# A recurrent two-layer block: scan items of one state by 1024 tokens, the drive in PSUM, C*h on GpSimd, and the experts' product on VectorE

## The reference

```python
# s: inner width 128, 64 states
A = -exp(A_log); delta = softplus(u @ W_delta + b_delta); Bm = u @ W_B; Cm = u @ W_C
def step(h, inputs):                      # u is silu(conv(left half of y @ W_up))
    dA = exp(d_t[..., None] * A)
    h = dA * h + (d_t * u_t)[..., None] * b_t[:, None, :]
    return h, einsum('bdn,bn->bd', h, c_t)
s = x + ((ys + u * D) * silu(right)) @ W_down + b_down
# m: 16 experts; each takes its 512 best tokens of each batch, and one shared expert takes all
h = gelu(x_tok @ Wg) * (x_tok @ Wu); eo = (h @ Wd) * topk_w   # scattered and added
```

## Time and profile before

| | us |
|---|---|
| median of 3 runs | 4562.25 |
| lowest and highest | 4562.19, 4566.79 |
| the profiled execution | 4572.77 |
| its span | 4571.0 |

### The profile page before, as it was taken

How to read it: one execution, slowest core, us unless ns; L and a number is a source line. 1 busy time by engine, 2 the same in 40 slices (tenths; PEclk the granted TensorE clock), 3 DMA queues, 4 the chain that set the end, 5 groups by cost and what they waited for, 6 DMA issues and landing times. The chain is left out here.

```text
span 4571.0 us, 63922 instructions
## 1 busy us (share of the span) xinstructions
PE 4084.4 (89%) x22996; PEld 3215.1 (70%) x22996; DVE 3323.2 (73%) x4687; ACT 2541.6 (56%) x4869; POOL 2382.1 (52%) x1652
## 2 busy tenths in 40 slices
PE   8899999979999999789999866689998999899975
PEld 7799999967899999656666545556666666566653
DVE  5466666655666666438788889888788787878777
ACT  6644444446444444367766643366666766666654
POOL 3100000032000000147667639789899998989887
PEclk9999999989999999899999858899999999999986
DMA  2010000010000000125444322455555565556568
GB/s 86 22 33 24 20 24 23 24 48 32 29 24 20 24 23 24 55 98 159 142 153 153 117 78 71 116 164 152 166 174 164 158 172 157 166 154 171 159 185 311
DMA packets 242095, 465.67 MB, mean 102 GB/s; under 512 B 33905, under 2 KB 154482, under 8 KB 241778
## 3 DMA queue, kind: packets, MB, share of 16 engines
q1 hardware_dynamic: 217202, 428.01, 29.2%
q0 software_dynamic: 24576, 33.57, 4.0%
HBM read 392.16 MB, written 69.34 MB: 101 GB/s over the span
## 5 line engine op out<-in xcount | busy, mean ns | idle before, releaser
L1560 POOL TENSOR_TENSOR scan_drive_sb<-scan_b_wide_sb,scan_du_sb 128x1024 f32<-128x1024 f32 x512 | 1304.7, 2567 | 241.4 <-DVE scan_h_sb L1472 234.7
L1472 DVE TENSOR_TENSOR_SCAN scan_h_sb<-decay_bank,scan_state_sb,scan_drive_sb 128x512 f32<-128x512 f32 x896 | 1107.7, 1267 | 135.8 <-ACT decay_bank L1810 125.8
L1810 ACT ACTIVATE decay_bank<-scan_delta_sb,a_neg_sb 128x512 f32<-128x512 f32 x1024 | 699.0, 686 | 263.8 <-DVE scan_h_sb L1472 261.0
L1479 DVE TENSOR_TENSOR scan_ch_sb<-c_pair,scan_h_sb 128x1024 f32<-128x1024 f32 x512 | 616.3, 1204 | 155.3 <-PE c_pair L1647 152.6
L1658 PEld LDWEIGHTS y_bank<-identity_sb,scan_ch_sb 128*128 128x128 f32 x4096 | 542.3, 151 | 191.1 <-issue 107.1
L1658 PE MATMUL y_bank<-identity_sb,scan_ch_sb 128*128 128x128 f32 x4096 | 641.3, 288 | 3.8 <-ACT scan_temp_sb L1828 3.8
L977 PE MATMUL ybank<-v_low_hi_lo_sb,pt_hi_b_sb 128*128 128x384 f32 x2048 | 622.1, 340 | 9.6 <-DVE pt_lo_b_sb L859 9.6
L912 POOL TENSOR_TENSOR acc_b_sb<-acc_b_sb,g_in_b_sb 128x256 f32<-128x256 f32 x64 | 47.2, 738 | 1101.2 <-DVE acc_b_sb L895 1101.2
L1647 PE MATMUL c_pair<-scan_cc_sb,select_state_sb 128*128 128x512 f32 x1024 | 445.1, 518 | 186.2 <-DVE scan_ch_sb L1479 185.3
L1014 ACT ACTIVATE p_b_sb<-scores,softmax_cols_b_sb 128x1024 f32<-128x1024 f32 x256 | 285.7, 1116 | 533.1 <-DVE softmax_cols_b_sb L853 395.9
L978 PE MATMUL ybank<-v_low_hi_lo_sb,pt_lo_b_sb 128*128 128x256 f32 x2048 | 574.2, 280 | 0.0
(11 more groups left out here) (302 smaller groups left out, 8112.7 us busy)
## 6 DMA issues: line engine op xcount, KB each, us to landing
scan_b_wide_sb<-b_scratch SPq DMA_DIRECT2D x512, 512.0 KB
x_b_sb<-x SPq DMA_DIRECT2D x16, 512.0 KB, 4.1
x_res_b_sb<-x SPq DMA_DIRECT2D x64, 128.0 KB, 2.3
g_in_b_sb<-g_scratch SPq DMA_DIRECT2D x64, 128.0 KB, 2.2
x_scratch<-x_res_b_sb SPq DMA_DIRECT2D x64, 128.0 KB, 1.7
xn_scratch<-xn_out_b_sb SPq DMA_DIRECT2D x64, 128.0 KB, 1.7
scan_xn_sb<-xn_scratch SPq DMA_DIRECT2D x16, 512.0 KB
moe_x_sb<-xn_scratch SPq DMA_DIRECT2D x16, 512.0 KB, 5.6
```

What stands on the lines that cost most here:

```text
L1472: e.tensor_tensor_scan(k.h[i % H_BUFFERS][:, j, :], k.decay_banks[S % DECAY_BANKS][:, :], k.drive[i % DRIVE_BUFFERS][:, j, :], start, ALU. ...
L1479: e.tensor_tensor(k.ch[i % CH_BUFFERS][:, :, :], k.c_bank[:, :, :], k.h[i % H_BUFFERS][:, :, :], ALU.mult).then_inc(k.s_ch, 1)
L1560: e.tensor_tensor(k.drive[i % DRIVE_BUFFERS][:, :, :], k.b_wide[i % B_BUFFERS][:, :, :], k.du[c % 2][:, :].unsqueeze(1).broadcast_to([P, P ...
L1810: e.activation(k.decay_banks[S % DECAY_BANKS][:, :], k.delta[c % 2][:, :], ACT.Exp, scale=wt.a[:, n:n + 1]).then_inc(k.s_decay, 1)
```

## The change

- An item is now one state of 1024 tokens (`WIDE`, two chunks): again 512 items, 64 per wide. Both chunks of a wide are prepared before its items begin.
- PE broadcasts B, no longer C: `broadcast_b(i + 1)` writes 1024 columns into one of two PSUM tiles of two banks each (`DRIVE_BANKS`), once the scan of item `i - 1` is over. DVE multiplies them in place by `delta * u` (`drive`) and runs one scan of 1024 columns, with the drive in PSUM and the decay in SBUF (three buffers, one exp of 1024 columns each). POOL does C*h (`read_out(i - 1)`), with C from DRAM, loaded two items ahead. PE's eight transposes of an item stand together.
- DVE makes the experts' product, with up read from PSUM; ACT's copy of the up part and POOL's product are gone, and h has two buffers.
- The projections of the scan use unsplit fp32 weights, one matmul for three, which removes the instructions that made the lower parts on ACT, DVE and POOL.
- The last two groups, not one, are finished after the scan; the others may come before. `down` runs for the two halves five steps apart.

```diff
+HALVES = 2
+WIDE = HALVES * CHUNK
+WIDES = ALL_CHUNKS // HALVES
+WIDES_OF = CHUNKS // HALVES
 INNER = 128
 STATES = 64
-PAIR = 2
-LAG = 2
-AHEAD = 2
-PAIRS = STATES // PAIR
-ITEMS = ALL_CHUNKS * PAIRS
+ITEMS = WIDES * STATES
+LAG = 3
...
-DECAY_BANKS = 3
+DECAY_BUFFERS = 3
+DRIVE_BANKS = 2
 H_BUFFERS = 3
 CH_BUFFERS = 2
-B_BUFFERS = 3
-DRIVE_BUFFERS = 3
-B_AHEAD = 4
+C_BUFFERS = 3
+C_AHEAD = 2
...
+def halves(prepare, W):
+    for half in range(HALVES):
+        yield from prepare(HALVES * W + half)
+
+
+def down_steps(step, W):
+
+    for s in range(DOWN_STEPS):
+        for half in range(HALVES):
+            if 0 <= s - HALF_LAG * half < HALF_STEPS:
+                step(HALVES * W + half, s - HALF_LAG * half)
+        yield
...
-        if 0 <= i - 1 < ITEMS:
-            broadcast_c(i - 1)
-        if 0 <= i + AHEAD < ITEMS:
-            drive(i + AHEAD)
-        for j in range(PAIR):
-            S = PAIR * i + j
-            if 0 <= S + 2 < PAIR * ITEMS:
-                decay(S + 2)
-            if 0 <= S < PAIR * ITEMS:
-                recur(S)
-            if 0 <= S - PAIR * LAG < PAIR * ITEMS:
-                add_up(S - PAIR * LAG)
-            if j == 0:
-                helpers.step()
-                yield
+            if m == LAG + C_AHEAD + 1 and W + 1 < WIDES:
+                helpers.ahead = halves(prepare, W + 1)
+            load_c(i + C_AHEAD)
+        if 0 <= i + 1 < ITEMS:
+            broadcast_b(i + 1)
+            decay(i + 1)
+        if 0 <= i < ITEMS:
+            drive(i)
+        helpers.step()
+        yield
+        if 0 <= i < ITEMS:
+            recur(i)
         if 0 <= i - 1 < ITEMS:
             read_out(i - 1)
             keep(i - 1)
-        if 0 <= i - LAG < ITEMS:
-            c, m = divmod(i - LAG, PAIRS)
-            if m == PAIRS - 1:
-                helpers.down.insert(0, down(c))
+        if 0 <= i - LAG + 1 < ITEMS:
+            add_up(i - LAG + 1)
+            W, m = divmod(i - LAG + 1, STATES)
+            if m == STATES - 1:
+                for half in range(HALVES):
+                    y_out(HALVES * W + half)
+                helpers.down.append(down_steps(down, W))
...
+    def load_c(i):
+        W, n = divmod(i, STATES)
+        w.wait_ge(k.s_c_saved, 16 * HALVES * (W + 1))
+        w.wait_ge(k.s_ch, i - C_BUFFERS + 1)
+        e.dma_start(k.c_wide[i % C_BUFFERS][:, :], c_dram[W][n, :].partition_broadcast(P)).then_inc(k.s_c[i % C_BUFFERS], 16)
...
-    def recur(S):
-        i, j = divmod(S, PAIR)
-        c, n = divmod(S, STATES)
-        w.wait_ge(k.s_decay, S + 1)
+    def drive(i):
+        W, n = divmod(i, STATES)
+        bank = k.drive_banks[i % DRIVE_BANKS][:, :]
+        w.wait_ge(k.s_b, i + 1)
+        w.wait_ge(k.s_du, HALVES * (W + 1))
+        e.tensor_tensor(bank, bank, k.du[W % 2][:, :], ALU.mult).then_inc(k.s_drive, 1)
+
+    def recur(i):
+        W, n = divmod(i, STATES)
+        w.wait_ge(k.s_decay, i + 1)
         w.wait_ge(k.s_drive, i + 1)
         w.wait_ge(k.s_kept, i - H_BUFFERS + 1)
         w.wait_ge(k.s_ch, i - H_BUFFERS + 1)
-        start = 0.0 if c % CHUNKS == 0 else k.state[:, n:n + 1]
-        e.tensor_tensor_scan(k.h[i % H_BUFFERS][:, j, :], k.decay_banks[S % DECAY_BANKS][:, :], k.drive[i % DRIVE_BUFFERS][:, j, :], start,
+        start = 0.0 if W % WIDES_OF == 0 else k.state[:, n:n + 1]
+        e.tensor_tensor_scan(k.h[i % H_BUFFERS][:, :], k.decay[i % DECAY_BUFFERS][:, :], k.drive_banks[i % DRIVE_BANKS][:, :], start,
                              ALU.mult, ALU.add).then_inc(k.s_scan, 1)
-
-    def read_out(i):
-        w.wait_ge(k.s_c, i + 1)
-        w.wait_ge(k.s_scan, 2 * (i + 1))
-        w.wait_ge(k.s_y, PAIR * (i - CH_BUFFERS + 1))
-        e.tensor_tensor(k.ch[i % CH_BUFFERS][:, :, :], k.c_bank[:, :, :], k.h[i % H_BUFFERS][:, :, :], ALU.mult).then_inc(k.s_ch, 1)
...
-    def drive(i):
-        c = i // PAIRS
-        w.wait_ge(k.s_b[i % B_BUFFERS], 16 * (i // B_BUFFERS + 1))
-        w.wait_ge(k.s_du, c + 1)
-        w.wait_ge(k.s_scan, PAIR * (i - DRIVE_BUFFERS + 1))
-        e.tensor_tensor(k.drive[i % DRIVE_BUFFERS][:, :, :], k.b_wide[i % B_BUFFERS][:, :, :],
-                        k.du[c % 2][:, :].unsqueeze(1).broadcast_to([P, PAIR, CHUNK]), ALU.mult).then_inc(k.s_drive, 1)
+    def read_out(i):
+        w.wait_ge(k.s_c[i % C_BUFFERS], 16 * (i // C_BUFFERS + 1))
+        w.wait_ge(k.s_scan, i + 1)
+        w.wait_ge(k.s_y, i - CH_BUFFERS + 1)
+        e.tensor_tensor(k.ch[i % CH_BUFFERS][:, :], k.c_wide[i % C_BUFFERS][:, :], k.h[i % H_BUFFERS][:, :], ALU.mult).then_inc(k.s_ch, 1)
...
-            e.matmul(bank, wt.up_hi[:, ci, cols], k.yt_hi[:, ci, :], start=(ci == 0), stop=False)
-            e.matmul(bank, wt.up_hi[:, ci, cols], k.yt_lo[:, ci, :], start=False, stop=False)
-            last = e.matmul(bank, wt.up_lo[:, ci, cols], k.yt_hi[:, ci, :], start=False, stop=(ci == DC - 1))
+            last = e.matmul(bank, wt.up[:, ci, cols], k.yt[:, ci, :], start=(ci == 0), stop=(ci == DC - 1))
...
-    def broadcast_c(i):
-        c, m = divmod(i, PAIRS)
-        fills.wait_emptied(w, "bc", c, 1)
-        w.wait_ge(k.s_ch, i)
-        for j in range(PAIR):
-            n = m * PAIR + j
-            last = e.matmul(k.c_bank[:, j, :], wt.select[:, n:n + 1].broadcast_to([P, P]), k.cc[c % 2][:, :], start=True, stop=True)
-        last.then_inc(k.s_c, 1)
-
-    def add_up(S):
-        i, j = divmod(S, PAIR)
-        c, n = divmod(S, STATES)
+    def broadcast_b(i):
+        W, n = divmod(i, STATES)
+        for half in range(HALVES):
+            fills.wait_emptied(w, "b", HALVES * W + half)
+        w.wait_ge(k.s_scan, i - DRIVE_BANKS + 1)
+        for half in range(HALVES):
+            cols = slice(half * CHUNK, (half + 1) * CHUNK)
+            last = e.matmul(k.drive_banks[i % DRIVE_BANKS][:, cols], wt.select[:, n:n + 1].broadcast_to([P, P]), k.bb[W % 2][:, cols],
+                            start=True, stop=True)
+        last.then_inc(k.s_b, 1)
+
+    def add_up(i):
+        W, n = divmod(i, STATES)
         w.wait_ge(k.s_ch, i + 1)
         if n == 0:
-            w.wait_ge(k.s_y_out, c)
-        for t in range(GT):
+            w.wait_ge(k.s_y_out, HALVES * W)
+        for t in range(HALVES * GT):
...
-    def decay(S):
-        c, n = divmod(S, STATES)
-        w.wait_ge(k.s_delta, c + 1)
-        w.wait_ge(k.s_scan, S - DECAY_BANKS + 1)
-        e.activation(k.decay_banks[S % DECAY_BANKS][:, :], k.delta[c % 2][:, :], ACT.Exp, scale=wt.a[:, n:n + 1]).then_inc(k.s_decay, 1)
+    def decay(i):
+        W, n = divmod(i, STATES)
+        w.wait_ge(k.s_delta, HALVES * (W + 1))
+        w.wait_ge(k.s_scan, i - DECAY_BUFFERS + 1)
+        e.activation(k.decay[i % DECAY_BUFFERS][:, :], k.delta[W % 2][:, :], ACT.Exp, scale=wt.a[:, n:n + 1]).then_inc(k.s_decay, 1)
...
-    def up(q, f):
-        fills.wait_filled(w, "moe_up", q, f)
-        w.wait_ge(k.s_h, HB * (q - 1) + f + 1)
-        e.activation(k.u[f][:, :], fills.bank("moe_up", q, f), ACT.Copy).then_inc(fills.emptied("moe_up", q, f), 1)
...
-    def product(q, f):
-        fills.wait_emptied(w, "moe_up", q, f)
-        w.wait_ge(k.s_gelu, HB * q + f + 1)
-        if q > 0:
-            wait_down(w, fills, q - 1)
-        e.tensor_tensor(k.h[:, f, :], k.u[f][:, :], k.g[f][:, :], ALU.mult).then_inc(k.s_h, 1)
...
+    def product(q, f):
+        fills.wait_filled(w, "moe_up", q, f)
+        w.wait_ge(k.s_gelu, HB * q + f + 1)
+        if q > 1:
+            wait_down(w, fills, q - 2)
+        e.tensor_tensor(k.h[q % 2][:, f, :], fills.bank("moe_up", q, f), k.g[f][:, :], ALU.mult).then_inc(fills.emptied("moe_up", q, f), 1)
...
-        w.wait_ge(k.s_h, HB * (q + 1))
+        wait_hidden(w, fills, q)
...
-LAST = ALL_GROUPS - 1
+LAST = ALL_GROUPS - HALVES
...
-        if g == LAST:
-            yield from no_steps(DOWN_STEPS)
+        while g >= LAST and not pace.scanned:
+            yield
```

493 lines of the change are left out of this document (211 added, 282 removed).

## The result

| | before | after |
|---|---|---|
| median of 4 runs each, us | 4562.22 | 4592.26 |
| lowest and highest | 4559.47, 4566.79 | 4590.19, 4596.14 |
| ratio, 95% interval | | 1.0067, 1.0054 to 1.0079 |

A forecast was written before the change was run, and what follows sets the result against it. No engine was full; engines holding each other up in turn set the pace. Start +44, shared -102, choice 0, routed -113, end +106, tail -12 total -77: span 4494, or 4485 us in the runs' measure, range 4370 to 4600.

The forecast's parts named there:

- The start: Before the first scan: both chunks of the first wide item prepared first, 31 more steps of 1.45 us, +44 us.
- the end: After the routed experts' last scatter: 40 items at 3.5 us plus final-group work and load waits, 174 us against 68, +106.
- the product: Gelu times up, moved to VectorE: next instruction starts 0.61 us later, +2.44 us per block, nothing hides it.
- rival (b): Scan on VectorE: the wide scan saves a fixed 0.2 us per 512-column scan, 102 us less, 4383 us; chance 0.04.
- T in the routed stage: Time of an item beside the routed experts: 41.8 us per block of 9.5 items, 4.4 us each against 4.70.
- the sentence on buffers: Two broadcast banks, three decay buffers, three of h: PE may be one whole item early, where the gain is expected.
- the floor: VectorE's undisturbed time per item, set by the scan: stays 3.48 us after the change, bounds 3.3 to 3.8.
- my sentences on what would prove me wrong: Slow wide scan or PSUM drive, VectorE waiting over 0.3 us per item at the product, or C*h holding PE's transposes.
- helper work: VectorE's other instructions in the routed stage: 1.1 us per block of 9.5 items.
- Rival (c): VectorE, between PE's up and down parts, becomes what everybody waits for: routed item 4.92 us, +139, 4700 us; chance 0.20.
- break-even of T = 4.6: From an item time of 4.6 us on, shorter stages no longer pay for the 138 us of start, end and tail.
- The choice: Choice of tokens: 43 items in both kernels, same chain between VectorE, ScalarE and PE, change 0.

The follow-up runs named there:

- x2: Changed kernel with the second half of each C*h on GpSimd left out (512 of 1024 columns): 4495.10 us.
- x4: Changed kernel with the transposes of C*h one item later (LAG 4) and three C*h buffers instead of two: 4575.12 us.
- x3: Changed kernel with half of the contraction of the experts' gate and up parts left out, one matmul in place of two: 4455.25 us.
- y4: Changed kernel with both the second half of C*h and half of the contraction of gate and up left out: 4355.19 us.
- x5: Changed kernel with the experts' product on GpSimd again, with ScalarE's copy of up and one moe_h: 4579.92 us.
- x11: Changed kernel with the drive written to two SBUF buffers instead of PE's bank, and two decay buffers instead of three: 5109.12 us.
- z1: Changed kernel with all of C*h but 16 columns left out: 4464.01 us.
- x8: Changed kernel with transposes an item later, three C*h buffers, and GpSimd's two double softplus steps made four single ones: 4578.65 us.
- x9: Changed kernel with the experts' product one step (half an item) later on VectorE: 4621.97 us.

## Why the prediction was wrong

**Right.** The start (+44), the end (+105 against +106) and the numbers of items in each stage; the wide scan (2.26 from start to start against 2.25); the product (0.58 against 0.61); the decay waits, 112 to 35 us; rival (b) did not come: the wide scan saves 0.10 us on two of 512, not 0.2. The prediction wrote that the trace has no scan of 1024 columns; it has two, in the choice of tokens (lines 2350 and 2364, 2.28 and 2.29 us), from which the term could have been read. The rule of the Trainium skill that the prediction weighed there (VectorE: DVE Perf Modes, section The DRAIN you can't avoid) has the trace against it still, as the prediction put it: the instruction behind the wide scan begins at 3871.16, 0.09 us before the scan's recorded end. The same section also says that an instruction that is not held starts earlier, and the prediction left that out.

**Wrong: DVE's idle time.** The step that failed is the one under *T in the routed stage*: "I leave 5.2 of the 8.7 us idle", and under it the sentence on buffers, "PE may be one whole item early. That is where I expect the gain." It measured 7.8, which over 33.5 blocks is 86 us of the 104 missed. About 1.0 of the 2.6 is a gap of 0.10 us between each drive and its scan (3868.80 to 3868.90 in the rows above), which the floor had at nothing: it took the overlap away and added no gap. The other 1.6, 54 us in the stage, is waiting. The prediction had taken each wait for itself: two banks halve the one for the broadcast, three decay buffers nearly end the one for decays. Both waits shrank, by 124 us in all. But by the order of their instructions DVE, GpSimd and PE were now tied in a ring that the kernel before did not have, where C*h was on DVE and GpSimd's drive ran ahead of the scan: scan, C*h behind the scatters, transposes, up part, product. Runs x2 and x4 show it at one place of the cycle, where two items get 54 us shorter when C*h is halved and about as much when C*h has an item more of time. For the whole stage the ring is argued: x3 and y4 show only that PE's and GpSimd's work both set the time and that their gains add. The usual lengths of a cycle's 19 items add up to 80.2 us before and 80.3 after, so the products and the new waits took all that the broadcast and the decays gave back. Of my sentences on what would prove me wrong, the last ("if GpSimd's C*h holds PE's transposes and through them the next broadcast") came true, with the up part beside the broadcast. GpSimd's fall from 90% to 78% busy had counted as relief; the mistake is that its instruction moved from ahead of the scan to behind it, and I called two items of `h` its slack, where PE's order and two C*h buffers left it less.

**Mis-sized: helper work.** The prediction put it at 1.1 us a block and gave no row for it. DVE's instructions in the routed stage other than drive, scan and product take 68.8 us, 2.1 a block (in the kernel before 2.5): 32 us more than forecast. Products (2.2 a block for 2.4) and the busy time of drive and scan (3.46 us an item for 3.48) give 14 back, and 86 + 32 - 14 are the 104. The item that nothing disturbs takes 3.56 us, not 3.48, since the drive is followed 1.32 us later by its scan where C*h was followed after 1.12, and the wide scan gives back only 0.10 of the 0.20 (the gap, already counted as idle, is in it).

**Rival (c)** came nearest: slower, by DVE standing between up part and down part. Its sizes were off as well: the product's wait was 0.19 us an item in the routed stage (61/318) and not 0.29, and T 4.73, not 4.92. Its break-even of T = 4.6 held: with 4.59 in the shared stage and 4.73 in the routed one the kernel is a little slower. Taking the product back (x5) wins 12 us, so the product is the smaller part; the one place at which C*h stands behind the scatters is worth 54.

**The choice** was 37 us shorter and not equal. That was luck: without it the span would be 131 us over its forecast and not 94. The traces show where some of it is. These are GpSimd and DVE of the kernel before, in one of the 30 rounds:

```profile
2602.47 2.36 POOL L1560 TENSOR_TENSOR scan_drive_sb<-scan_b_wide_sb,scan_du_sb 128x1024 f32<-128x1024 f32 x1 [2.86 <-DVE scan_h_sb L1472]
2603.53 1.30 DVE L2333 TENSOR_TENSOR bits_sb<-bits_sb,step_sb 128x1 int32<-128x1 int32 x1
```

This instruction of one column, with both operands in SBUF, takes 0.16 us in 17 of the rounds, and here 1.30, until GpSimd's drive ends at 2604.83: it is the standstill of x11 again. The 30 of these take 18.6 us in the kernel before and 4.8 in the changed one, where each got in before C*h; 32 comparisons of 1024 columns (`moe_x_sb`, line 2396) take 56.9 and 40.3. That is 30 us less of DVE's time, with some 9 more in other instructions of this kind; how much of it the stage waited for was not tried. With C*h left out (z1) the choice takes 272 us, with half of it (x2) 282, so GpSimd's load matters there too, and the ring needn't be the way: the 17 us of x2 match those by which DVE's 32 instructions of line 2331 (two SBUF operands) got shorter, 45.7 to 28.6.

**Open.** The items of the preparation. Over their usual length in the two-block cycle they cost 9 us per 19 items before and after alike; in x4 and x8 it is 11. The 22 us that the shared stage missed were not taken apart.

## What to carry to other kernels

When work moves to another engine, ask first whether it now runs ahead of the critical engine or behind it, and only then how busy that engine is: in the kernel before VectorE waited 2.3 us in the whole routed stage for GpSimd's drive, which ran ahead; C*h, an instruction of about the same length behind the scan, gave 97 us when it was halved and 128 when it was left out. (The drive was not left out in the kernel before, so this compares a wait with a run.) Waits read from a profile are not a sum of separate prices; draw the ring of who waits for whom in the changed order, and price a buffer only by the wait that comes next (x4: -17; x9: +30). Two operands of a VectorE instruction in SBUF are a tie to GpSimd that no semaphore shows, and that makes even an instruction of one column wait.

## What the runs showed of the hardware

- A scan of 1024 columns with both operands in SBUF took 3.29 us beside C*h on GpSimd, with one operand in PSUM 2.35, and 2.36 to 2.48 again with C*h narrowed. The cost was 517 us in one kernel.
- The same tie is in both kernels in smaller places: the instruction that forms delta (L1434, two SBUF operands, 512 columns) takes 1.93 us in the routed stage (2.32 in the kernel before, line 1439), and 0.68 in z1, where C*h is narrow. In the choice of the kernel before an instruction of one column takes 1.30 us beside GpSimd's drive and 0.16 otherwise.
- Writing the drive to PSUM costs what writing to SBUF costs: 1.21 and 1.20 us for 1024 columns. A scan that waits for the product of 1.22 us just in front of it on VectorE starts 1.32 us after that one's start; the scan behind C*h of 1.20 us, which doesn't wait for it, starts after 1.12.
